# Strip copies in two halves, lower maxima first, and a projection held over into the next group

## The reference, cut to what matters

```python
q = split_heads(x @ Wq.T + bq)
k = split_heads(x @ Wk.T + bk)
v = split_heads(x @ Wv.T + bv)
q_lr = jnp.einsum('bhtd,hdr->bhtr', q, Wq_lsr)
k_lr = jnp.einsum('bhtd,hdr->bhtr', k, Wk_lsr)
scores = jnp.einsum('bhir,bhjr->bhij', q_lr, k_lr) * scale
scores = jnp.where(causal_mask, -jnp.inf, scores)
attn = jax.nn.softmax(scores, axis=-1)
y = jnp.einsum('bhij,bhjd->bhid', attn, v)
```

## Time and profile before

| | us |
|---|---|
| median of 3 executions | 4002.01 (3996.65 to 4010.14) |
| profiled execution, its own time | 4006.51 |
| its span | 4004.8 |
| TensorE busy | 3661.8 (91%) |
| VectorE busy | 2291.9 (57%) |
| ScalarE busy | 1476.8 (37%) |
| GpSimd busy | 658.8 (16%) |
| first score of the first sequence | at 147.30 |
| one sequence (418.87 to 692.50) | 273.6 |
| of it the tail (635.69 to 692.50) | 56.8 |

### The profile page before, as it was taken

How to read it: one execution, slowest core, us unless ns; L and a number is a source line. 1 busy time by engine, 2 the same in 40 slices (tenths; PEclk the granted TensorE clock), 3 DMA queues, 4 the chain that set the end, 5 groups by cost and what they waited for, 6 DMA issues and landing times. The chain is left out here.

```text
span 4004.8 us, 56465 instructions
## 1 busy us (share of the span) xinstructions
PE 3661.8 (91%) x20457; PEld 2508.7 (63%) x20457; DVE 2291.9 (57%) x5022; ACT 1476.8 (37%) x2763; POOL 658.8 (16%) x852
## 2 busy tenths in 40 slices
PE   4899999999999999999999716799999999999995
PEld 3555555555555555555555306688888888888884
DVE  2576665765665666656657376344544444445456
ACT  1243443443444434434434302333333333333335
POOL 2022121121121221211211200011111111111113
PEclk7999999999999999999999855899999999999997
DMA  5134233233433351433233200433444333334458
GB/s 164 43 106 133 60 96 117 50 105 101 107 81 88 88 143 49 107 106 74 82 101 75 75 0 6 145 117 121 124 128 123 119 117 116 121 117 128 123 167 307
DMA packets 188919, 423.54 MB, mean 106 GB/s; under 512 B 39840, under 2 KB 42912, under 8 KB 180512
## 3 DMA queue, kind: packets, MB, share of 16 engines
q1 hardware_dynamic: 162032, 367.97, 29.9%
q0 software_dynamic: 14400, 35.14, 4.4%
q10 hardware_dynamic: 12288, 17.83, 1.5%
HBM read 246.75 MB, written 72.38 MB: 80 GB/s over the span
## 5 line engine op out<-in xcount | busy, mean ns | idle before, releaser
L795 ACT ACTIVATE probs<-scores_t 128x512 f32<-128x512 f32 (+3 forms) x1536 | 662.3, 497 | 618.3 <-PE scores_t L665 564.9
L1717 PE MATMUL m_ps_h<-m_tokens_t,m_w_parts 128*128 128x512 f32 x3072 | 740.6, 391 | 1.6 <-DVE m_tokens_t L1599 1.6
L1717 PE MATMUL m_ps_y<-m_w_parts,m_hidden_parts 128*128 128x512 f32 x3072 | 737.4, 390 | 0.6
L1717 PEld LDWEIGHTS m_ps_y<-m_w_parts,m_hidden_parts 128*128 128x128 f32 x3072 | 575.4, 188 | 125.8 <-issue 6.2
L1717 PEld LDWEIGHTS m_ps_h<-m_tokens_t,m_w_parts 128*128 128x128 f32 x3072 | 576.1, 188 | 120.3 <-issue 2.0
L851 DVE CUSTOM_DVE_ANT_0 shared_banks<-shared_banks,mask_q_rows 128x128 f32<-128x128 f32 (+3 forms) x1024 | 478.9, 514 | 252.5 <-PE shared_banks L622 247.3
L622 PE MATMUL shared_banks<-k_operands,q_operands 96*128 96x512 f32 (+3 forms) x1536 | 501.9, 385 | 42.5 <-DVE max_slots L851 17.9
L665 PE MATMUL scores_t<-q_operands,k_operands 128*128 128x512 f32 (+3 forms) x1536 | 489.2, 376 | 35.1 <-ACT probs L795 27.0
L622 PEld LDWEIGHTS shared_banks<-k_operands,q_operands 96*128 96x128 f32 x1536 | 280.0, 191 | 302.1 <-issue 115.3
L1535 ACT ACTIVATE m_hidden<-m_ps_h,m_b 128x512 f32<-128x512 f32 x256 | 176.6, 690 | 792.1 <-PE m_ps_h L1717 779.0
L528 POOL TENSOR_SCALAR_AFFINE_SELECT probs<-probs 128x256 f32<-128x256 f32 x512 | 219.9, 432 | 1374.7 <-ACT probs L795 1373.9
(11 more groups left out here) (218 smaller groups left out, 3211.9 us busy)
## 6 DMA issues: line engine op xcount, KB each, us to landing
m_w_raw<-in_w1T SPq DMA_DIRECT2D x64, 1024.0 KB, 5.2
m_w_raw<-in_w2T SPq DMA_DIRECT2D x64, 1024.0 KB, 7.5
q_operands<-natural SPq DMA_DIRECT2D x384, 128.0 KB, 2.5
k_operands<-natural SPq DMA_DIRECT2D x384, 128.0 KB, 2.5
wqk_group<-scratch_wqk SPq DMA_DIRECT2D x32, 1024.0 KB, 6.0
natural<-in_xT SPq DMA_DIRECT2D x8, 2048.0 KB, 9.5
x_residual<-in_x ACTq DMA_DIRECT2D x64, 256.0 KB, 2.9
scratch_x<-probs SPq DMA_DIRECT2D x64, 256.0 KB, 2.2
```

What stands on the lines that cost most here:

```text
L795: act.activation(probs[:, slot_of(k, h // 2), h % 2, c0:HALF], st[:, (HG * k + h) % SCORE_BANKS, c0:HALF], ACT.Exp, scale=SCALE).then_inc( ...
L1717: mm = pe.matmul(bank, a, b, start=(first and n == 0), stop=(final and n == len(pairs) - 1))
```

## The change

It has these parts:

- The strips go in two parts, columns 0 to 511 (lower) and 512 to 1023 (upper), with 24 copies each of 32 rows of 2 KB. The lower part may leave when projections 0 and 1 are out of their banks and step 7 has read the lower columns for the last time; the upper part when projections 2 and 3 are out and the last step is read. Semaphores: lower_sent for each pair of heads, upper_sent for each head.
- The projections change order: first queries and keys of the lower half, then of the upper half.
- Projection 3 of slots 0, 1 and 2 is issued after place 2 of the next slot. Slot 3 keeps its own.
- The maxima begin with the four lower pieces of each head (16 in all), then eight upper pieces per head; their places now begin at 1 instead of 9.
- Projection 2 goes from place 56 to 57. The reciprocals of the first half stand at 30, 36, 42, 45, of the second half at 2, 6, 10, 14 of the slot that follows.
- Some one-off semaphores (ident_ready, zeroed) are merged into others.

```diff
     for h in range(HG):
         out += [(h, it, it, 0, (it + 1) * P) for it in range(4)]
+    for h in range(HG):
         out += [(h, it, it, 0, HALF) for it in range(4, TT)]
         out += [(h, it + 4, it, HALF, (it + 1) * P - HALF) for it in range(4, TT)]
...
-MAX_AFTER = (0, 0, 0, 0, 0, 0, 0, 0, 0, 2, 2, 1, 1, 0, 3, 0, 0, 0, 3, 0,
-             2, 0, 3, 1, 0, 0, 2, 0, 1, 2, 0, 1, 2, 1, 2, 0, 0, 2, 1, 1,
-             0, 2, 2, 4, 1, 0, 1, 2, 1, 0, 1, 1, 0, 0, 0, 0, 0, 0, 0, 0)
-PROJ_AFTER = (46, 47, 56, 57)
+MAX_AFTER = (0, 3, 0, 1, 1, 1, 2, 1, 1, 2, 0, 0, 0, 0, 0, 2, 1, 0, 1, 1,
+             1, 0, 2, 1, 1, 0, 1, 1, 1, 1, 2, 0, 1, 2, 2, 0, 0, 2, 1, 0,
+             2, 1, 2, 1, 0, 2, 0, 1, 1, 0, 2, 0, 0, 0, 0, 0, 0, 0, 0, 0)
+PROJ_AFTER = (46, 47, 57, 57)
+HELD_AFTER = 2
...
-INVERT_AFTER = ((30, 42, 45, 45), (0, 4, 4, 5))
+INVERT_AFTER = ((30, 36, 42, 45), (2, 6, 10, 14))
+LOWER_READ_AT = 7
...
-        order += [("proj", g, i) for i, at in enumerate(PROJ_AFTER) if at == n]
+        held = 3 if g < GROUPS - 1 else 4
+        order += [("proj", g, i) for i, at in enumerate(PROJ_AFTER[:held]) if at == n]
+        if g > 0 and n == HELD_AFTER:
+            order.append(("proj", g - 1, 3))
...
-            for i in (2, 3):
+            for i in (2 * part, 2 * part + 1):
...
-                for h in range(HG):
-                    sp.wait_ge(strips_sent[h], n * STRIPS)
+                for part, each in zip((lower_sent, upper_sent), ALL_SENT):
+                    for semaphore in part:
+                        sp.wait_ge(semaphore, n * each)
...
-                        plain(sp, st_full, (b * GROUPS + slot + 1) * NE * HG, sp_passed)
+                        read = (b * GROUPS + slot) * NE + (NE if part else LOWER_READ_AT + 1)
+                        plain(sp, st_full, read * HG, sp_passed)
+                cols = slice(part * HALF, (part + 1) * HALF)
...
-                        sp.dma_start(raw(q_ops[dst, g % 2, h, :]), nat[src, Q_STRIPS[s], :]).then_inc(strips_sent[h], 16)
-                        sp.dma_start(raw(k_ops[dst, g % 2, h, :]), nat[src, 2 + K_STRIPS[s], :]).then_inc(strips_sent[h], 16)
+                        sp.dma_start(raw(q_ops[dst, g % 2, h, cols]), nat[src, Q_STRIPS[s], cols]).then_inc(sent[part][h], 16)
+                        sp.dma_start(raw(k_ops[dst, g % 2, h, cols]), nat[src, 2 + K_STRIPS[s], cols]).then_inc(sent[part][h], 16)
...
-                    strips(b, slot)
+                    strips(b, slot, 0)
+                    strips(b, slot, 1)
...
-                    strips(b, GROUPS - 2)
+                    strips(b, GROUPS - 2, 0)
+                    strips(b, GROUPS - 2, 1)
                     load_w(1)
+                    strips(b, GROUPS - 1, 0)
                 for t in range(TT):
                     store(b, t)
                     if more and t < HG:
-                        strips(b, GROUPS - 1, heads=(t,))
+                        strips(b, GROUPS - 1, 1, heads=(t,))
...
-            strips(0, GROUPS - 2, True)
-            strips(0, GROUPS - 1, True)
+            for slot in (GROUPS - 2, GROUPS - 1):
+                strips(0, slot, 0, True)
+                strips(0, slot, 1, True)
...
-                        which, hh = i // 2, i % 2
+                        hh, which = i // 2, i % 2
...
-                        if item[2] % 12 == 0:
-
-                            pe.wait_ge(strips_sent[h], (1 if lead else nxt + g + 1) * STRIPS)
+                        if item[2] < LOWER_PIECES and item[2] % (LOWER_PIECES // 2) == 0:
+                            pe.wait_ge(lower_sent[h // 2], (1 if lead else nxt + g + 1) * 2 * STRIPS)
+                        if item[2] >= LOWER_PIECES and item[2] % UPPER_PIECES == 0:
+                            pe.wait_ge(upper_sent[h], (1 if lead else nxt + g + 1) * STRIPS)
```

More of the change, by code:

```diff
@@ L185, in max_steps @@
     return out
+LOWER_PIECES = 4 * HG
+UPPER_PIECES = 8
 PROB_BUFS = 4
@@ L326, in build_attention @@
         masked = sem("masked")
-        consts, strip_zero, strips_filled, own_zeros, ident_ready = sem("consts"), sem("strip_zero"), sem("strips_filled"), sem("own_zeros"), sem("ident_ready")
+        consts, strip_zero, strips_filled, own_zeros = sem("consts"), sem("strip_zero"), sem("strips_filled"), sem("own_zeros")
         x_in, x_split, w_in = sem("x_in"), sem("x_split"), sem("w_in")
@@ L331, in build_attention @@
         sp_passed, pool_passed, dve_passed = sem("sp_passed"), sem("pool_passed"), sem("dve_passed")
-        strips_sent = [sem(f"strips_sent{h}") for h in range(HG)]
+        lower_sent = [sem(f"lower_sent{h}") for h in range(0, HG, 2)]
+        upper_sent = [sem(f"upper_sent{h}") for h in range(HG)]
         st_full, exp_done, pv_done, normed = sem("st_full"), sem("exp_done"), sem("pv_done"), sem("normed")
@@ L344, in build_attention @@
         STRIPS = 16 * 2 * len(Q_STRIPS)
+        sent = ([lower_sent[h // 2] for h in range(HG)], upper_sent)
+        ALL_SENT = (2 * STRIPS, STRIPS)
         steps, maxes = attend_steps(), max_steps()
@@ L400, in seen_by, with await_parts @@
             return (last_seen if b == NB - 1 else batch_seen)[item]
-        def await_parts(eng, passed, b, g, lead=False):
+        def await_parts(eng, passed, b, g, part, lead=False):
             _, at, off = scope(b, lead)
-            for i in (2, 3):
+            for i in (2 * part, 2 * part + 1):
                 bank, turn = at[("proj", g, i)]
@@ L427, in load_w, with strips @@
                 sp.dma_start(raw(wqk[:]), scratch["wqk"][g].rearrange("p (k c n) -> p k c n", k=4, c=DC)).then_inc(w_in, 16)
-            def strips(b, slot, lead=False, heads=range(HG)):
+            def strips(b, slot, part, lead=False, heads=range(HG)):
                 g = (slot + AHEAD) % GROUPS
                 if 0 in heads:
-                    await_parts(sp, sp_passed, b, slot, lead)
+                    await_parts(sp, sp_passed, b, slot, part, lead)
                     if not lead:
-                        plain(sp, st_full, (b * GROUPS + slot + 1) * NE * HG, sp_passed)
+                        read = (b * GROUPS + slot) * NE + (NE if part else LOWER_READ_AT + 1)
+                        plain(sp, st_full, read * HG, sp_passed)
+                cols = slice(part * HALF, (part + 1) * HALF)
                 for h in heads:
@@ L486, in _ @@
                     sp.dma_start(rb[q * DH:q * DH + E_N, :], w["rb"].rearrange("(e a) -> e a", a=1)).then_inc(router_in, 16)
-            await_parts(sp, sp_passed, 0, GROUPS - 2, True)
+            await_parts(sp, sp_passed, 0, GROUPS - 2, 0, True)
+            await_parts(sp, sp_passed, 0, GROUPS - 2, 1, True)
             load_w(1)
-            strips(0, GROUPS - 2, True)
-            strips(0, GROUPS - 1, True)
+            for slot in (GROUPS - 2, GROUPS - 1):
+                strips(0, slot, 0, True)
+                strips(0, slot, 1, True)
             load_w(2)
@@ L509, in _ @@
             pool.affine_select(out=ident[:], in_=ident[:], compare_op=ALU.not_equal, fill=1.0, base=0,
-                               pattern=[[-1, P]], channel_multiplier=1).then_inc(ident_ready, 1)
-            pool.wait_ge(ident_ready, 1)
+                               pattern=[[-1, P]], channel_multiplier=1).then_inc(own_zeros, 1)
+            pool.wait_ge(own_zeros, 3)
             pool.affine_select(out=mask_q[:, HALF - P:HALF], in_=mask_q[:, HALF - P:HALF], compare_op=ALU.is_ge,
@@ L729, in run @@
                             if not lead or g == GROUPS - 1:
-                                for h in range(HG):
-                                    act.wait_ge(strips_sent[h], (1 if lead else b * GROUPS + g + AHEAD) * STRIPS)
+                                for part, each in zip((lower_sent, upper_sent), ALL_SENT):
+                                    for semaphore in part:
+                                        act.wait_ge(semaphore, (1 if lead else b * GROUPS + g + AHEAD) * each)
                         gn = (g + AHEAD) % GROUPS
@@ L1323, in build_experts @@
         h_full, gelu_done, h_hi, h_lo, fc2_done = sem("h_full"), sem("gelu_done"), sem("h_hi"), sem("h_lo"), sem("fc2_done")
[L1324 to L1325 removed]
+        y_copied, out_ready, scattered, consts = (sem("y_copied"), sem("out_ready"), sem("scattered"), sem("m_consts"))
         z_in = [sem(f"f_in{b}") for b in range(Z_BUFS)]
@@ L1446, in _ @@
             pool.memset(eps[:], EPS).then_inc(eps_ready, 1)
-            pool.memset(ident[:], 0.0).then_inc(zeroed, 1)
-            pool.wait_ge(zeroed, 1)
+            pool.memset(ident[:], 0.0).then_inc(consts, 1)
+            pool.wait_ge(consts, 1)
             pool.affine_select(out=ident[:], in_=ident[:], compare_op=ALU.not_equal, fill=1.0, base=0,
@@ L1513, in token_hi @@
                 act.activation(xe[:, r, HI, c, :], ps_t[:, c % 2, 0:CAP], ACT.Copy).then_inc(xe_hi, 1)
-            act.wait_ge(consts, 1)
+            act.wait_ge(consts, 2)
```

(2 more changed lines are left out.)

2 lines of the change are left out of this document (removed).

## The result

The change makes the kernel slower: 4049.5 us median (4044.87 to 4051.28, four executions) against 3999.33 (3996.02 to 4010.14), a ratio of 1.0119 with a 95% interval of 1.0097 to 1.0141. The profiled execution took 4051.28 us, 44.8 more than that of before. Forecast were 4015, in a range of 3965 to 4055, from a median of 4002 for the kernel before: 0.3% slower, where 1.2% was measured. The sign is right, the size is not, and the likeliest case's own range (4002 to 4030) was missed.

The account below looks back on a forecast made before the run. TensorE, busy 91% of the span, was taken as the bound. Slots 1 and 3 +3, slot 0 -18, slot 2 +15 and lead-in +13 gave +13 us on 4006.5, 4019.5, so 4015 against the median; range 3965 to 4055.

Parts of the forecast that it names:

- The sign: Whole kernel: predicted slower, by 0.3%; slower by over 0.3% was given chance 0.45.
- likeliest case: Whole kernel: the forecast itself, without any rival, 4002 to 4030 us, chance 0.45.
- The strips' price: SP's strip copies: half copies still leave every 0.63 us, landing after 2.3 us; 0.32 if bytes alone count.
- Rival A: Strip copies: smaller copies leave faster, 0.55 us apart; sum -24 us, 3978, or 3939 at 0.32 us; chance 0.15.
- The lead-in: Before the first group: 48 strip copies instead of 24 delay the start, +13 us once (bound +7).
- Slot 0: First group slot of each sequence: nine maxima lie under the eight exponentials, 8 x -2.3 = -18 us.
- Slot 2: Third slot: the next sequence's x lands later behind 48 copies and ScalarE waits longer, 7 x 2.1 = +15 us.
- Slots 1 and 3: Slots starting with a held projection: later first weigh, fewer maxima afterwards; net +0.2 each, +3 us in all.
- Rival C: Slot starts: VectorE's queue behind the held projection is worse, +1.5 in each of 22 slots; 4053 us; chance 0.15.
- Rival B: All slots: spreading maxima shortens bank waits, 1.3 us more from each of 31 slots; 3975 us; chance 0.15.

Follow-up runs that it names:

- old_places: Changed kernel with projection 3 back in its own slot and maxima, projections and reciprocals at their earlier places; strips stay halved, lower pieces first: 4044.26 us, 1.0113.
- lead_whole: Changed kernel with only the lead-in's strips sent whole again, 24 copies a group: 4033.71 us, 1.0094 of the kernel before.
- before_slot0: Kernel before the change, with the maxima at the change's places in slot 0 alone, strips whole: 3985.64 us, 0.9964.
- fill: Changed kernel plus ten matmuls of 512 columns, result unread, among the first maxima of slots 1 to 3: 4035.99 us, 1.0093 of the kernel before.
- no_hold: Changed kernel with projection 3 back at the end of its own slot; early maxima and halved strips stay: 4055.31 us, 1.0139 of the kernel before.
- late_reciprocals: Changed kernel with the second half's reciprocals at places 10, 11, 12, 14 instead of 2, 6, 10, 14: 4060.14 us, 1.0149 of the kernel before.
- eight_later: Changed kernel with maximum 8, the first needing strips of heads 2 and 3, moved behind the first weigh: 4047.86 us, 1.0126 of the kernel before.
- free_start: Changed kernel with projection 3 in its own slot, reciprocals at 10 to 14 and maximum 8 behind the first weigh: 4021.88 us, 1.006 of the kernel before.
- free_start_x_lead: free_start with the lead-in's strips whole and the next sequence's x loaded ahead of slot 0's projection weights: 3999.26 us, 0.9999 of the kernel before.

## Why the prediction was right, and where it was off

**The strips' price: right.** Taken were 0.63 us for a half copy, against 0.32 if bytes set it; the rows show 0.63, with landing at 2.0 instead of 2.3. Rival A, which needed 0.57 or less, is out. old_places shows what it costs with nothing placed early: 39 us of slot 2 and lead-in (the order of pieces included).

**The lead-in: right.** +13 forecast, +11.7 in the trace, and lead_whole gives 12.4 back. Over all runs the first score comes at 158.0 to 162.4 with the lead-in in halves (seven kernels) and at 144.3 to 149.7 with it whole (six), so the term is known to a few us only.

**Slot 0: right.** -2.3 each forecast (with the projection near 46.5), -1.9 measured, 46.81. before_slot0 gets 1.7 of it without any halved copy.

**Slot 2: right in mechanism, forecast too small.** +15 forecast, +20 measured. x is issued 25.3 us after the slot's start and not 24.3, lands 34.9 after it, and ScalarE waits 4.70 (5.3 forecast). The wait at the first maximum, 0.3 us in slot 1, is 0.98 in slot 3 of sequence 1, and the clock is 0.92, not 0.94.

**Slots 1 and 3: the step that failed, by its size.** "Net +0.2, over 8 slots 1 and 7 slots 3: **+3 us** (bounds -0.7 and +1.5 each)" measured +24. The waits and their order were as forecast, and the weigh started after 8.9 to 10.5 us for 9.3. Where the clock held, the lengths were right too: slot 1 51.99 and 52.46 (52.3 forecast), slot 3 54.78 (55). It held in two of eight slots 1 and one of seven slots 3. The other six slots 1 average 54.2, the other six slots 3 57.4: 2.0 and 2.6 us more, 28 us in all. Some 20 of these are the clock's. From the first weigh to step 4 the three slots take 6.9 us, the twelve 8.0 to 9.5, and nothing behind step 4 differs. The other 8 are later weighs (0.4 us later in slot 1, 0.8 in slot 3, on average). The working had TensorE's idle at the start grow from 1.9 to 3.7 us and priced it as idle alone; the clock it had in slot 2 only. fill shows the link: with the waits filled by work that nobody needs the clock is kept, and the kernel gains 13.5 us. The page "TensorE: Matmul & The Clock Gate" of the Trainium skill (A second HAM failure mode: psum-queue depth-cycling) describes this form, an array that falls to its lower clock because it idles briefly and often between groups of matmuls; this trace agrees, as no wait listed at that start is longer than 0.94 us. Where the clock holds and where it does not among equal slots, no row here explains: sequences 4 and 5 start their weighs after 8.92 and 8.89 us, and only the second keeps the clock.

**Rival C has the size, not the mechanism.** It gave 4053 for VectorE's queue behind the held projection, and the upper end of the range, 4055, was drawn for it. That 4049.5 lies inside is therefore luck: the cause that brought it there was not the one that the range allowed for. no_hold, without that projection, is no faster, and late_reciprocals, with a freer queue, starts its weighs no sooner. Nor does eight_later, against the strip at maximum 8, gain. Each of these waits covers the next; only with all of them gone does the start shorten to 3.7 us, and 28 us come back. My expectations of no_hold and eight_later had taken the wait that a row names for the only one standing there.

**Rival B: wrong.** The waits of TensorE's weight loads for VectorE in the kernel after, for the earlier trace rows; the second line is the unmasked pieces, for which before had 6.9 us in 31:

```profile
PEld shared_banks L644 <- DVE max_slots L874: 66.4, 167, 1.2
PEld shared_banks L644 <- DVE max_slots L878: 47.6, 126, 0.8
```

114 us in all, where it was 117: the spread moved these waits and hardly shortened them.

**Still open.** free_start's slots are 52 us although its start is as short as before's with eight maxima already done. From the first weigh to step 4 it takes 8.3 to 9.7 us where the clock held, for 8.8 before with more of the maxima still to do. The wait for the 24th strip explains 1.6 us of this; the rest lies in smaller idle pieces that I did not separate. Open too is why late_reciprocals kept the clock in ten of fifteen slots with a start as long as the changed kernel's.

## What to carry to other kernels

Where the issue of copies limits a burst, as here, halving them pays only if the issue gets cheaper; look for a smaller copy of the same kind in the trace before the split, and multiply its issue time by the new count. When several waits end within a few microseconds of each other, taking one away proves little: the next one stands at the same place, so the price of an early start is that of the slowest of them, here the 24th copy of a queue at 0.63 us each. And idle time that is planned into a TensorE-bound stretch can have a second price, the clock of the matmuls behind it (here 1.0 to 2.5 us in twelve of fifteen slots). So take an early start where its inputs have long landed, as in slot 0.

## What the runs showed of the hardware

- A copy of 32 rows from SBUF to SBUF leaves SP every 0.63 us with 64 KB as with 128 KB; only landing fell, from 2.5 to 2.0 us (medians).
- TensorE's granted clock fell after a stretch of 9.7 us in which it was busy for 7.3 and no listed wait was over 0.94 us; the eight matmuls of the weigh then took 1.94 us instead of 1.06. With 9.1 busy of 10.4 us (fill) it held, and after 8.9 us (sequences 4 and 5) it once fell and once held.
- The 2 MB load of x landed 7.4 to 11.5 us after its issue with a 1 MB load of weights issued 1.4 to 3.6 us ahead of it, mostly 9.2 to 10.3, and 7.3 to 8.8 us, mostly 7.4, with that load behind it.
- In free_start_x_lead the clock fell behind a single wait of 1.57 us for a strip; in free_start it held behind one of 1.63.
